# The first weights of a mixture-of-experts kernel: a transfer of its own for chunk 1, and two transfers issued by ScalarE

## The chip, the cores and the metric

One core of one Trainium2 chip. The metric is the device time of the kernel in microseconds (us); lower is better. Everything here happens once, in the first 11 us of about 309.

## The reference

Two steps on x of shape (16, 128, 128), with residuals. The first is a mixture of 8 routed experts and a shared one, each a gated pair of projections; the second multiplies each of the 16 blocks from the left with one of 100 matrices, chosen by a step number.

```python
g = einsum('bsd,edf->ebsf', h, Wg);  u = einsum('bsd,edf->ebsf', h, Wu)
expert_outs = einsum('ebsf,efd->ebsd', silu(g) * u, Wd)          # 8 experts, D = 128, F = 512
expert_output = einsum('be,ebsd->bsd', gating_probs, expert_outs)
shared = einsum('bsf,fd->bsd', silu(h @ Sg) * (h @ Su), Sd)
x = x + (1 - sg) * expert_output + sg * shared
x = x + einsum('bij,bjk->bik', T[steps - 1], x)
```

## The kernel before

The 16 blocks are four tiles `t` of 4 blocks, each 128 x 512 (`W` = 512) with D on the partitions. The 512 hidden features of an expert are four chunks `c` of 128. A unit `n` is one chunk of one expert for one tile: `project_g` and `project_u` make a 128x512 bank each, ScalarE takes SiLU of the first (`silu`), VectorE multiplies (`make_h`), and two units later (`LAG` = 2) `project_down` adds the chunk's part to an output bank. 9 experts x 4 tiles x 4 chunks are 144 units, expert by expert, tile by tile, chunk by chunk.

Each product is made of three matmuls: every operand is split into a rounded high part (`_hi`) and a rest (`_lo`), and hi·hi, hi·lo and lo·hi are added. So a unit is 9 matmuls of 128x512 and the splits are work for the other engines: the high part is a copy to the type fp32r, and the low part is the difference. In the loop GpSimd splits the weights of the next expert. Expert 0 has no expert ahead of it, and its split is written out by hand:

- SyncE issues, in this order: tile 0 of x; gate and up weights of chunk 0 (`W_gu0`, 128 KB); gate and up weights of chunks 1 to 3 (`W_gu`, 384 KB); all down weights (`W_d0`, 256 KB); tile 1 of x; the side values; tiles 2 and 3 of x; all of expert 1.
- ScalarE loads its table, runs one activation on a zero (so that the table is there), rounds chunk 0 (semaphore `w0_rounded` 1), chunk 1 (`w0_rounded` 2), takes SiLU of unit 0, and rounds the down weights (`w0_rounded` 3).
- VectorE rounds and splits tile 0 of x, makes the low part of chunk 1 and the high part of chunks 2 and 3 (`split_done` 3, which is `EARLY`).
- GpSimd makes the low parts of chunk 0, chunk 2, chunk 3 and the down weights, in this order, and counts them in `w_ready` 1 to 4.
- TensorE runs 8 matmuls on a tile of zeros (`warm_up`), then unit 0 (`opening`, each of hi·hi, lo·hi and hi·lo for gate and up), unit 1, and from unit 2 the loop, in which it waits for `w_ready` 2 ahead of unit 2, and for `w_ready` 4 ahead of the first `project_down`.

All engines run their own list in order and wait on semaphores. Nothing is scheduled by a program.

Of the kernel before, what the change touches and what calls it, by code (L numbers as in the profile page):

```python
# [5 lines left out]
P = 128  # L6
F32 = mybir.dt.float32
# [5 lines left out]
def moe_then_step_kernel(  # L13
# [3 lines left out]
    step: bass.AP,  # L17
    W_gu0: bass.AP,
    W_gu: bass.AP,
    W_d0: bass.AP,  # L20
# [8 lines left out]
    NC = W_all.shape[2]  # L29
# [10 lines left out]
    LAG = 2  # L40
# [16 lines left out]
    with ExitStack() as ctx:  # L57
# [3 lines left out]
        def sem(name):  # L61
            return ctx.enter_context(nc.semaphore(name))

        zero = sb("zero", [P, P])
        x_hi = sb("x_hi", [P, NT, W], F32R)
        x_lo = sb("x_lo", [P, NT, W], F32R)
        w_raw = sb("w_raw", [P, 2, NC, 3, P])
        w_hi = sb("w_hi", [P, 2, NC, 3, P], F32R)
# [17 lines left out]
        g_bank = [ctx.enter_context(nc.psum_tensor(f"g_bank{i}", [P, W], F32)) for i in range(2)]  # L86
# [3 lines left out]
        x_in = [sem(f"x_in{i}") for i in range(3)]  # L90
        wc0_in = [sem(f"wc0_in{i}") for i in range(2)]
        wd0_in = sem("wd0_in")
# [52 lines left out]
        def _(sp):  # L145
# [6 lines left out]
            load_x(0, 1, x_in[0])  # L152
            sp.dma_start(w_raw[:, 0, 0, 0:2, :], W_gu0[:, :, :]).then_inc(wc0_in[0], 16)
            sp.dma_start(w_raw[:, 0, 1:NC, 0:2, :], W_gu[:, :, :, :]).then_inc(wc0_in[1], 16)
            sp.dma_start(w_raw[:, 0, :, 2, :], W_d0[:, :, :]).then_inc(wd0_in, 16)
# [42 lines left out]
        def _(pool):  # L198
# [5 lines left out]
            def low_part(slot, c, m):  # L204

                return nc.gpsimd.tensor_tensor(w_lo[:, slot, c, m, :], w_raw[:, slot, c, m, :],  # L206
                                               w_hi[:, slot, c, m, :].bitcast(F32), ALU.subtract)
# [7 lines left out]

            pool.wait_ge(w0_rounded, 1)
            low_part(0, 0, slice(0, 2)).then_inc(w_ready, 1)
            pool.wait_ge(split_done, EARLY)
            low_part(0, 2, slice(0, 2)).then_inc(w_ready, 1)
            low_part(0, 3, slice(0, 2)).then_inc(w_ready, 1)  # L220
            pool.wait_ge(w0_rounded, 3)
            low_part(0, slice(0, NC), 2).then_inc(w_ready, 1)

# [57 lines left out]
        def _(act):  # L281
# [22 lines left out]
            def round_w0(c, m):  # L304
                nc.scalar.activation(w_hi[:, 0, c, m, :], w_raw[:, 0, c, m, :], ACT.Copy).then_inc(w0_rounded, 1)  # L305

            act.wait_ge(zero_done, 1)
            nc.scalar.activation(silu_0[:, :], zero[:, 0:1], ACT.Silu)
            for c in range(2):
                act.wait_ge(wc0_in[c], 16)  # L310
                round_w0(c, slice(0, 2))
            silu(0, 0)
# [26 lines left out]
        def _(dve):  # L339
# [30 lines left out]
            def copy_result(i):  # L370
# [9 lines left out]
            nc.vector.tensor_tensor(x_lo[:, 0, :], acc[:, 0, :], x_hi[:, 0, :].bitcast(F32), ALU.subtract).then_inc(split_done, 1)  # L380
            dve.wait_ge(w0_rounded, 2)
            nc.vector.tensor_tensor(w_lo[:, 0, 1, 0:2, :], w_raw[:, 0, 1, 0:2, :], w_hi[:, 0, 1, 0:2, :].bitcast(F32),
                                    ALU.subtract).then_inc(split_done, 1)
            dve.wait_ge(wc0_in[1], 16)
            nc.vector.tensor_copy(w_hi[:, 0, 2:NC, 0:2, :], w_raw[:, 0, 2:NC, 0:2, :]).then_inc(split_done, 1)
# [45 lines left out]
        def _(pe):  # L431
# [64 lines left out]
            def warm_up(n):  # L496

                for _ in range(n):
                    nc.tensor.matmul(o_bank[1][:, 0:P], zero[:, :], zero[:, :], start=True, stop=True)

            pe.wait_ge(zero_done, 1)
            warm_up(8)

            def opening(x_part, w_part, start, stop):
                for bank, m in ((g_bank[0], 0), (u_bank[0], 1)):
                    last = nc.tensor.matmul(bank[:, :], w_part[:, 0, 0, m, :], x_part[:, 0, :], start=start, stop=stop)
                    if stop:
                        last.then_inc(u_done if m else g_done, 1)

            pe.wait_ge(x_rounded, 1)  # L510
            pe.wait_ge(w0_rounded, 1)
            opening(x_hi, w_hi, True, False)
            pe.wait_ge(split_done, 1)
            opening(x_lo, w_hi, False, False)
            pe.wait_ge(w_ready, 1)
            opening(x_hi, w_lo, False, True)
            pe.wait_ge(w0_rounded, 2)
            nc.tensor.matmul(g_bank[1][:, :], w_hi[:, 0, 1, 0, :], x_hi[:, 0, :], start=True, stop=False)
# [4 lines left out]
            with pe.Fori(0, E - 2, 2) as e:  # L523
                for k in range(LAG, 2 * U + LAG):

                    if k in (2, 3):
                        pe.wait_ge(w_ready, k)
                    if k % U == 0:
                        pe.wait_ge(w_ready, NC * (e + k // U + 1))
                    if k in range(NC, U, NC):  # L530
                        pe.wait_ge(acc_done, k // NC)
                    project_g(e * U + k, k, place(k))
                    project_u(e * U + k, k, place(k))
                    if k == LAG:

                        pe.wait_ge(w_ready, NC)
                    project_down(e * U + k - LAG, k - LAG, place(k - LAG))
# [77 lines left out]
```

## Time and profile before

| | us |
|---|---|
| time before, median of 3 runs | 308.99 (308.96 to 309.49) |
| the profiled execution: its own time | 309.61 |
| the profiled execution: its span in the trace | 307.8 |
| TensorE (PE) busy | 303.3 of 307.8 |

The trace is of one execution. Its span runs from the first to the last record; 1.81 us of the execution's own time lie around it. PE is the matmul, PEld TensorE's load of weights (it overlaps PE), DVE is VectorE, ACT ScalarE, POOL GpSimd, SPq SyncE's queue of DMA issues. Matmuls are pipelined: a 128x512 matmul is shown with about 0.39 us, while the next one starts 0.23 us after it; the distance of starts is the one to count.

### The profile page before, as it was taken

To read this page: it belongs to the slowest core of one execution; us is meant where nothing else is said; L and a number is where in the kernel's file an instruction comes from. 1 tells how busy PE (TensorE), PEld (TensorE's weight loads), DVE (VectorE), ACT (ScalarE), POOL (GpSimd) and SP (SyncE) were. 2 spreads that over 40 slices of the span, in tenths; PEclk is the share of its full clock that TensorE was granted. 3 is DMA by queue.
4 is the path that set the end of the run, shared out by engine and by line. 5 is a ranking of instruction groups with operands and counts; after the bars stand their busy time and mean duration, and the time that the engine had idled before them with its cause. 6 is when DMAs were issued, how large, how long until landed. Compare 5 with 4: busy or idle time off the path is not lost.

```text
span 307.8 us, 4474 instructions
## 1 busy us (share of the span) xinstructions
PE 303.3 (99%) x1348; PEld 251.0 (82%) x1348; DVE 214.4 (70%) x350; ACT 162.4 (53%) x301; POOL 102.5 (33%) x116
## 2 busy tenths in 40 slices
PE   8999999999999999999999999999999999999996
PEld 7788888888888888888888888888888888888885
DVE  2667766776676666776677667776676667787974
ACT  4665555555555555555555555555555555554562
POOL 2675212441155115511542134411451155710010
PEclk9999999999999999999999999999999999999999
DMA  7600300030002000020003000003000000013242
GB/s 201 252 2 0 103 1 2 0 102 0 1 0 86 16 0 0 6 97 0 0 0 111 26 26 26 19 25 111 0 0 2 0 0 0 2 34 68 39 101 102
DMA packets 13882, 12.00 MB, mean 39 GB/s; under 512 B 6960, under 2 KB 11952, under 8 KB 13872
## 3 DMA queue, kind: packets, MB, share of 16 engines
q1 hardware_dynamic: 13872, 11.87, 12.6%
q8 instruction: 6, 0.10, 0.1%
q14 instruction: 4, 0.03, 0.0%
HBM read 10.04 MB, written 1.84 MB: 39 GB/s over the span
## 4 chain that ended last, share of the span: by engine, by line
PE 95%; DMA 2%; POOL 1%; DVE 1%; SPq 0%; issue 0%; ACT 0%
PE o_bank L461 11%; PE o_bank L464 11%; PE o_bank L462 11%; PE g_bank L434 10%; PE u_bank L434 10%; PE g_bank L436 10%; PE u_bank L436 10%; PE g_bank L435 10%; PE u_bank L435 10%; DMA w_raw<-in_W_gu 2%; POOL w_lo L206 1%; PE o_bank L479 1%; DVE res L373 1%; PE g_bank L479 0%; PE u_bank L474 0%
## 5 line engine op out<-in xcount | busy, mean ns | idle before, releaser
L344 DVE TENSOR_TENSOR u_bank<-u_bank,silu_g 128x512 f32<-128x512 f32 x144 | 100.7, 699 | 83.4 <-PE u_bank L436 83.3
L286 ACT ACTIVATE silu_g<-g_bank 128x512 f32<-128x512 f32 x144 | 86.1, 598 | 134.3 <-PE g_bank L436 134.2
L249 POOL TENSOR_TENSOR acc<-acc,scaled 128x512 f32<-128x512 f32 x32 | 41.5, 1298 | 183.4 <-DVE scaled L358 183.2
L350 DVE TENSOR_TENSOR h_lo<-u_bank,h_hi 128x512 fp32r<-128x512 f32 x144 | 97.9, 680 | 0.1
L292 ACT ACTIVATE h_hi<-u_bank 128x512 fp32r<-128x512 f32 x144 | 85.4, 593 | 0.4 <-DVE u_bank L344 0.4
L461 PE MATMUL o_bank<-h_hi,w_hi 128*128 128x512 f32 x144 | 56.2, 390 | 0.2 <-POOL w_lo L206 0.2
L464 PE MATMUL o_bank<-h_lo,w_hi 128*128 128x512 f32 x144 | 56.0, 389 | 0.0
L462 PE MATMUL o_bank<-h_hi,w_lo 128*128 128x512 f32 x144 | 56.0, 389 | 0.0
L436 PE MATMUL u_bank<-x_hi,w_lo 128*128 128x512 f32 x143 | 55.6, 389 | 0.0
L434 PE MATMUL u_bank<-x_hi,w_hi 128*128 128x512 f32 x143 | 55.6, 389 | 0.0
L435 PE MATMUL u_bank<-x_lo,w_hi 128*128 128x512 f32 x143 | 55.6, 389 | 0.0
L434 PE MATMUL g_bank<-x_hi,w_hi 128*128 128x512 f32 x142 | 55.4, 390 | 0.0
L435 PE MATMUL g_bank<-x_lo,w_hi 128*128 128x512 f32 x142 | 55.3, 389 | 0.0
L436 PE MATMUL g_bank<-x_hi,w_lo 128*128 128x512 f32 x142 | 55.2, 389 | 0.0
L206 POOL TENSOR_TENSOR w_lo<-w_raw,w_hi 128x384 fp32r<-128x384 f32 (+2 forms) x36 | 36.2, 1009 | 7.9 <-ACT w_hi L305 2.8
L461 PEld LDWEIGHTS o_bank<-h_hi,w_hi 128*128 128x128 f32 x144 | 27.0, 188 | 6.1 <-POOL w_lo L206 0.6
L464 PEld LDWEIGHTS o_bank<-h_lo,w_hi 128*128 128x128 f32 x144 | 27.0, 188 | 5.7
L462 PEld LDWEIGHTS o_bank<-h_hi,w_lo 128*128 128x128 f32 x144 | 27.0, 188 | 5.5
L434 PEld LDWEIGHTS g_bank<-x_hi,w_hi 128*128 128x128 f32 x142 | 26.7, 188 | 5.9 <-ACT silu_g L286 0.5
L436 PEld LDWEIGHTS u_bank<-x_hi,w_lo 128*128 128x128 f32 x143 | 26.8, 188 | 5.6
L435 PEld LDWEIGHTS u_bank<-x_lo,w_hi 128*128 128x128 f32 x143 | 26.8, 188 | 5.6
L434 PEld LDWEIGHTS u_bank<-x_hi,w_hi 128*128 128x128 f32 x143 | 26.8, 188 | 5.5
(58 smaller groups left out, 143.9 us busy)
## 6 DMA issues: line engine op xcount, KB each, us to landing
w_raw<-in_W_all SPq DMA_DIRECT2D x8, 768.0 KB, 4.4
T_plus<-in_TT SPq DMA_DIRECT2D x16, 64.0 KB, 1.7
turned_y<-yB SPq DMA_DIRECT2D x3, 256.0 KB, 2.3
y<-turned_y SPq DMA_DIRECT2D x12, 64.0 KB, 2.3
out_y<-res SPq DMA_DIRECT2D x3, 256.0 KB, 2.2
acc<-in_xT SPq DMA_DIRECT2D x2, 256.0 KB, 3.8
acc<-in_xT SPq DMA_DIRECT2D x1, 512.0 KB, 6.7
w_raw<-in_W_gu SPq DMA_DIRECT2D x1, 384.0 KB, 4.8
```

What stands on the lines that cost most here:

```text
L206: return nc.gpsimd.tensor_tensor(w_lo[:, slot, c, m, :], w_raw[:, slot, c, m, :], w_hi[:, slot, c, m, :].bitcast(F32), ALU.subtract)
L249: nc.gpsimd.tensor_tensor(acc[:, t, :], acc[:, t, :], scaled[:, t % 2, :], ALU.add).then_inc(acc_done, 1)
L286: nc.scalar.activation(silu_g[:, k % 2, :], g_bank[k % 2][:, :], ACT.Silu).then_inc(g_read, 1)
L292: nc.scalar.activation(h_hi[:, k % HR, :], u_bank[k % HR][:, :], ACT.Copy).then_inc(h_rounded, 1)
L344: nc.vector.tensor_tensor(u_bank[k % HR][:, :], u_bank[k % HR][:, :], silu_g[:, k % 2, :], ALU.mult).then_inc(h_done, 1)
L350: nc.vector.tensor_tensor(h_lo[:, k % HR, :], u_bank[k % HR][:, :], h_hi[:, k % HR, :].bitcast(F32), ALU.subtract).then_inc(split_done, 1)
L434: nc.tensor.matmul(bank, w_hi[:, w[0], w[1], w[2], :], x_h, start=start, stop=False)
L435: nc.tensor.matmul(bank, w_hi[:, w[0], w[1], w[2], :], x_l, start=False, stop=False)
L436: return nc.tensor.matmul(bank, w_lo[:, w[0], w[1], w[2], :], x_h, start=False, stop=stop)
L461: nc.tensor.matmul(bank[:, :], w_hi[:, w[0], w[1], w[2], :], h_hi[:, slot, :], start=c == 0, stop=False)
L462: nc.tensor.matmul(bank[:, :], w_lo[:, w[0], w[1], w[2], :], h_hi[:, slot, :], start=False, stop=False)
L464: last = nc.tensor.matmul(bank[:, :], w_hi[:, w[0], w[1], w[2], :], h_lo[:, slot, :], start=False, stop=c == NC - 1)
```

## The change

Chunk 1 gets a tensor and a transfer of its own, and `W_gu` shrinks to chunks 2 and 3. ScalarE issues the transfer of chunk 0 and that of chunks 2 and 3 itself, ahead of its table load; SyncE issues x tile 0, chunk 1, the down weights and the rest. Chunk 0 is rounded in two halves (gate, then up), and the first two matmuls wait for one half each, so that every later count of `w0_rounded` is one more. GpSimd makes the low part of the down weights ahead of that of chunk 3, and TensorE's waits follow: `w_ready` 2 ahead of unit 2, 3 ahead of the first `project_down`, 4 ahead of unit 3. The warm-up matmuls read a constant zero, which the program's preamble sets on GpSimd, and no longer wait for VectorE's `zero`.

```diff
@@ SyncE
             load_x(0, 1, x_in[0])
-            sp.dma_start(w_raw[:, 0, 0, 0:2, :], W_gu0[:, :, :]).then_inc(wc0_in[0], 16)
-            sp.dma_start(w_raw[:, 0, 1:NC, 0:2, :], W_gu[:, :, :, :]).then_inc(wc0_in[1], 16)
+            sp.dma_start(w_raw[:, 0, 1, 0:2, :], W_gu1[:, :, :]).then_inc(wc0_in[1], 16)
             sp.dma_start(w_raw[:, 0, :, 2, :], W_d0[:, :, :]).then_inc(wd0_in, 16)
@@ GpSimd
-            pool.wait_ge(w0_rounded, 1)
+            pool.wait_ge(w0_rounded, 2)
             low_part(0, 0, slice(0, 2)).then_inc(w_ready, 1)
             pool.wait_ge(split_done, EARLY)
             low_part(0, 2, slice(0, 2)).then_inc(w_ready, 1)
+            pool.wait_ge(w0_rounded, 4)
+            low_part(0, slice(0, NC), 2).then_inc(w_ready, 1)
             low_part(0, 3, slice(0, 2)).then_inc(w_ready, 1)
-            pool.wait_ge(w0_rounded, 3)
-            low_part(0, slice(0, NC), 2).then_inc(w_ready, 1)
@@ ScalarE
+            act.dma_start(w_raw[:, 0, 0, 0:2, :], W_gu0[:, :, :]).then_inc(wc0_in[0], 16)
+            act.dma_start(w_raw[:, 0, 2:NC, 0:2, :], W_gu[:, :, :, :]).then_inc(wc0_in[2], 16)
             act.wait_ge(zero_done, 1)
             nc.scalar.activation(silu_0[:, :], zero[:, 0:1], ACT.Silu)
-            for c in range(2):
-                act.wait_ge(wc0_in[c], 16)
-                round_w0(c, slice(0, 2))
+            act.wait_ge(wc0_in[0], 16)
+            for m in range(2):
+                round_w0(0, m)
+            act.wait_ge(wc0_in[1], 16)
+            round_w0(1, slice(0, 2))
@@ VectorE
-            dve.wait_ge(w0_rounded, 2)
+            dve.wait_ge(w0_rounded, 3)
...
-            dve.wait_ge(wc0_in[1], 16)
+            dve.wait_ge(wc0_in[2], 16)
@@ TensorE
-                    nc.tensor.matmul(o_bank[1][:, 0:P], zero[:, :], zero[:, :], start=True, stop=True)
-
-            pe.wait_ge(zero_done, 1)
+                    nc.tensor.matmul(o_bank[1][:, 0:P], nought, nought, start=True, stop=True)
+
+            nought = nc.const_aps.tensor(0.0, (P, P), F32)
             warm_up(8)
...
-            pe.wait_ge(w0_rounded, 1)
-            opening(x_hi, w_hi, True, False)
+            for bank, m in ((g_bank[0], 0), (u_bank[0], 1)):
+                pe.wait_ge(w0_rounded, m + 1)
+                nc.tensor.matmul(bank[:, :], w_hi[:, 0, 0, m, :], x_hi[:, 0, :], start=True, stop=False)
...
-                    if k in (2, 3):
-                        pe.wait_ge(w_ready, k)
+                    if k == LAG:
+                        pe.wait_ge(w_ready, 2)
+                    if k == LAG + 1:
+                        pe.wait_ge(w_ready, NC)
...
                     if k == LAG:
-                        pe.wait_ge(w_ready, NC)
+                        pe.wait_ge(w_ready, 3)
                     project_down(e * U + k - LAG, k - LAG, place(k - LAG))
```

The first place is the start of ScalarE's list. Before (`in_W_gu0` is chunk 0, `w_hi<-w_raw` the rounding of weights, `silu_g<-g_bank` the SiLU of a unit):

```order
L308 ACT_TABLE_LOAD
L308 ACTIVATE silu_0<-zero 128x1 [waits zero_done]
L305 ACTIVATE w_hi<-w_raw 128x256 [waits wc0_in0]
L305 ACTIVATE w_hi<-w_raw 128x256 [waits wc0_in1]
L286 ACTIVATE silu_g<-g_bank0 128x512 [waits g_done]
L305 ACTIVATE w_hi<-w_raw 128x4x128 [waits wd0_in]
L286 ACTIVATE silu_g<-g_bank1 128x512 [waits g_done]
```

And after the change:

```order
L307 DMA w_raw<-in_W_gu0 128x256
L308 DMA w_raw<-in_W_gu 128x2x256
L310 ACT_TABLE_LOAD
L310 ACTIVATE silu_0<-zero 128x1 [waits zero_done]
L305 ACTIVATE w_hi<-w_raw 128x128 [waits wc0_in0]
L305 ACTIVATE w_hi<-w_raw 128x128
L305 ACTIVATE w_hi<-w_raw 128x256 [waits wc0_in1]
L286 ACTIVATE silu_g<-g_bank0 128x512 [waits g_done]
L305 ACTIVATE w_hi<-w_raw 128x4x128 [waits wd0_in]
L286 ACTIVATE silu_g<-g_bank1 128x512 [waits g_done]
```

Two DMA issues now stand ahead of the table load, and the rounding of chunk 0 is two instructions.

The second place is GpSimd's list from its first low part (`w_lo<-w_raw,w_hi`) on. Before, the four rows are chunk 0, chunk 2, chunk 3 and the down weights (128x4x128):

```order
L206 TENSOR_TENSOR w_lo<-w_raw,w_hi 128x256 [waits w0_rounded]
L206 TENSOR_TENSOR w_lo<-w_raw,w_hi 128x256 [waits split_done]
L206 TENSOR_TENSOR w_lo<-w_raw,w_hi 128x256
L206 TENSOR_TENSOR w_lo<-w_raw,w_hi 128x4x128 [waits w0_rounded]
L227 TENSOR_TENSOR x_lo<-acc,x_hi 128x512 [waits x_rounded]
```

And after the change:

```order
L206 TENSOR_TENSOR w_lo<-w_raw,w_hi 128x256 [waits w0_rounded]
L206 TENSOR_TENSOR w_lo<-w_raw,w_hi 128x256 [waits split_done]
L206 TENSOR_TENSOR w_lo<-w_raw,w_hi 128x4x128 [waits w0_rounded]
L206 TENSOR_TENSOR w_lo<-w_raw,w_hi 128x256
L227 TENSOR_TENSOR x_lo<-acc,x_hi 128x512 [waits x_rounded]
```

The down weights' row has moved up past chunk 3's, so chunk 3 now also stands behind ScalarE's rounding of the down weights.

## Rows read from the trace of the kernel before

**Rows 1.** Busy time by stretch (PE, PEld, DVE, ACT, POOL), granted clock, DMA share, GB/s.

```profile
4.50:10.53 6.03, 5.48 (x20) 3.49 (x20) 2.96 (x7) 3.90 (x8) 3.53 (x5) 1.00 0.99 333
10.53:303.69 293.16, 293.16 (x1306) 243.08 (x1307) 208.82 (x338) 156.10 (x289) 98.08 (x106) 1.00 0.10 30
```

**Rows 2.** Who PE waited for from 11 us (of 308) on: total, times, longest.

```profile
PE o_bank L461 <- POOL w_lo L206: 0.2, 1, 0.2
```

**Rows 3.** Timeline of TensorE, 0 to 11 us: start, duration, what, wait before.

```profile
1.06 3.78 PE L499 MATMUL o_bank<-zero 128*128 128x128 f32 x16 [1.06 <-DVE zero L376]
...
4.50 0.77 PE L506 MATMUL g_bank<-x_hi,w_hi 128*128 128x512 f32 x1
...
5.07 0.63 PE L506 MATMUL u_bank<-x_hi,w_hi 128*128 128x512 f32 x1
...
5.50 0.48 PE L506 MATMUL g_bank<-x_lo,w_hi 128*128 128x512 f32 x1
...
6.05 0.40 PE L506 MATMUL g_bank<-x_hi,w_lo 128*128 128x512 f32 x1
...
6.28 0.39 PE L506 MATMUL u_bank<-x_hi,w_lo 128*128 128x512 f32 x1
...
6.97 0.50 PE L518 MATMUL g_bank<-x_hi,w_hi 128*128 128x512 f32 x1 [0.29 <-ACT w_hi L305]
...
8.67 0.49 PE L434 MATMUL g_bank<-x_hi,w_hi 128*128 128x512 f32 x1
...
10.53 0.50 PE L461 MATMUL o_bank<-h_hi,w_hi 128*128 128x512 f32 x1 [0.21 <-POOL w_lo L206]
```

**Rows 4.** The chain that ended last, 0 to 11 us: start, duration, what.

```profile
1.66 4.82 DMA w_raw<-in_W_gu
...
7.29 0.43 DVE w_hi L385
...
7.79 2.70 POOL w_lo L206 x3
```

**Rows 5.** Timeline of the other engines, 0 to 11 us.

```profile
0.75 1.28 ACT L308 ACT_TABLE_LOAD   x1 [0.75 <-PEq L604]
...
3.54 0.43 DVE L378 CAST x_hi<-acc 128x512 fp32r<-128x512 f32 x1 [2.53 <-DMA acc<-in_xT]
...
3.83 0.42 ACT L305 ACTIVATE w_hi<-w_raw 128x256 fp32r<-128x256 f32 x1 [1.58 <-DMA w_raw<-in_W_gu]
4.00 0.69 DVE L380 TENSOR_TENSOR x_lo<-acc,x_hi 128x512 fp32r<-128x512 f32 x1
...
7.30 0.62 ACT L305 ACTIVATE w_hi<-w_raw 128x512 fp32r<-128x512 f32 x1
```

**Rows 6.** Timeline of SyncE's issues: start, duration of the issue.

```profile
1.18 0.43 SPq L153 DMA_DIRECT2D w_raw<-in_W_gu  x1
...
1.66 0.64 SPq L154 DMA_DIRECT2D w_raw<-in_W_gu  x1
...
2.34 0.61 SPq L155 DMA_DIRECT2D w_raw<-in_W_d  x1
```

**Rows 7.** DMA issues, 0 to 12 us: KB each, us from issue to landing.

```profile
w_raw<-in_W_gu SPq DMA_DIRECT2D x1, 384.0 KB, 4.8
w_raw<-in_W_d SPq DMA_DIRECT2D x1, 256.0 KB, 4.9
w_raw<-in_W_gu SPq DMA_DIRECT2D x1, 128.0 KB, 2.6
```

**Rows 8.** GpSimd's low parts of weights, 0 to 12 us: ns min/median/max.

```profile
L206 POOL TENSOR_TENSOR w_lo<-w_raw,w_hi x4: 736/850/1290, 4.3 to 9.2; 128x256 fp32r<-128x256 f32 x3, 128x512 fp32r<-128x512 f32 x1
```

**Rows 9.** The page, costliest groups: busy us, mean ns of one, idle before.

```profile
L286 ACT ACTIVATE silu_g<-g_bank 128x512 f32<-128x512 f32 x144 | 86.1, 598 | 134.3 <-PE g_bank L436 134.2
```

**Rows 10.** Busy time by stretch, as rows 1; last column GB/s.

```profile
2.50:3.00 0.50, 0.50 (x5) 0.50 (x4) 0.00 (x0) 0.00 (x0) 0.00 (x0) 1.00 1.04 387
...
3.50:4.00 0.50, 0.50 (x4) 0.50 (x3) 0.43 (x1) 0.17 (x1) 0.00 (x0) 1.00 0.81 154
```

More of the change, by code:

```diff
@@ L18, in moe_then_step_kernel @@
     W_gu0: bass.AP,
+    W_gu1: bass.AP,
     W_gu: bass.AP,
@@ L90, in moe_then_step_kernel @@
         x_in = [sem(f"x_in{i}") for i in range(3)]
-        wc0_in = [sem(f"wc0_in{i}") for i in range(2)]
+        wc0_in = [sem(f"wc0_in{i}") for i in range(3)]
         wd0_in = sem("wd0_in")
@@ L516, in _ @@
             opening(x_hi, w_lo, False, True)
-            pe.wait_ge(w0_rounded, 2)
+            pe.wait_ge(w0_rounded, 3)
             nc.tensor.matmul(g_bank[1][:, :], w_hi[:, 0, 1, 0, :], x_hi[:, 0, :], start=True, stop=False)
@@ L597 @@
         "W_gu0": routed[0, :, 0, 0:2],
-        "W_gu": routed[0, :, 1:, 0:2],
+        "W_gu1": routed[0, :, 1, 0:2],
+        "W_gu": routed[0, :, 2:, 0:2],
         "W_d0": routed[0, :, :, 2],
```

## The prediction, made before the changed kernel ran

> **What bounds the kernel now.** I read the table by stretch first. From 10.53 us to 303.69 TensorE is busy for 293.16 of 293.16 us [rows 1], and the only wait that the list of waits gives it from 11 us on is one of 0.2 us that belongs to the matmul at 10.53 [rows 2]. So the middle has a fixed length, and what the start gains, the whole kernel gains, if nothing behind it is tied to the clock on the wall instead of to TensorE. In the stretch ahead, 4.50 to 10.53, there is something to gain: 6.03 us [rows 1], for 18 matmuls (units 0, 1 and 2). At full pace they start 0.23 us apart, as 6.28 does after 6.05 [rows 3], which makes 4.1 us. The other 1.9 us are lost.
>
> The chain that ended last says who is to blame: the 384 KB transfer of chunks 1 to 3 from 1.66 to 6.48, behind it VectorE's cast of chunks 2 and 3 at 7.29, then three low parts on GpSimd for 2.70 us, until 10.49 [rows 4]. The timeline of TensorE shows where the 1.9 us lie. Its first two matmuls start 0.57 and 0.43 us apart (4.50, 5.07, 5.50), against 0.23 later [rows 3]; the granted clock reads 1.00 in this stretch [rows 1] and doesn't show this, but the same shape at twice the distance is the 1.2 GHz level against 2.4. The pace changes between 5.50 and 6.05. The four distances from 4.50 to 6.05 are 1.55 us against 0.92: 0.6 us for the low clock. Then 6.28 to 6.97 is 0.46 too long (chunk 1 wasn't there), with another 0.1 behind it; unit 2 starts at 8.67, 0.2 late with 0.1 behind it, for GpSimd's chunk 2; and 10.53 is 0.38 late, for GpSimd's last low part [rows 3]. The idle pieces sum to 1.26 us.
>
> **The start of the first matmul.** The warm-up runs from 1.06 for 3.4 us, up to 4.50, and it waited for VectorE's zero tile until 1.06 [rows 3]. ScalarE's list starts at 0.75 [rows 5]; TensorE's would start about then too, so the warm-up, if it costs the same, ends at 4.2 instead of 4.5: 0.30 us. That the same 8 matmuls on a constant that is read again and again are no slower, no row shows; I take them as equal, bounded by nothing gained at all (0) and the full 0.3. Is the first operand there at 4.2? x tile 0 landed at 3.54, its cast takes 0.43, so 3.97 [rows 5]. Chunk 0 landed 2.6 us after its issue at 1.18 [rows 6, 7]; issued at 0.75 by ScalarE that is 3.35. ScalarE itself has to issue twice (0.43 and at most 0.64, from SyncE's rows [rows 6]) and load its table (1.28 [rows 5]), which ends at 3.1, plus the activation on one column, about 3.35. Then two halves; a whole 256 takes 0.42 [rows 5], so the gate half is there by 3.7 and the up half by 4.0. I count 0.30.
>
> **The clock.** If the rise stays at about 5.65 us, starting 0.3 earlier only buys 0.3 us at half pace, 0.15 of it is lost again. If it moves with the warm-up, nothing is. The row shows one rise, 4.6 us after the first warm-up matmul [rows 3]. The Trainium skill, "TensorE: Matmul & The Clock Gate", section "What's actually happening", says that the chip's activity monitor doesn't restart with the kernel and that the moment of the rise varies by some 500 ns from run to run. By that rule the rise keeps no distance to the warm-up, and the sum would be 1.4 instead of 1.55, with a scatter of 0.25 us around it; one trace can't tell.
>
> **Chunk 1.** Alone it is 128 KB, issued second by SyncE at 1.18; the 128 KB that stood there landed after 2.6 us, at 3.8 [rows 6, 7]; at worst 4.8 as the 384 KB did, at 6.0. Rounding is 0.42. From 4.2, 3.4 matmuls at half pace bring TensorE to 5.65, and the rest of unit 0 to 6.25. So chunk 1 may land at 5.8 without being felt, and the 0.56 us of idleness there goes.
>
> **Chunks 2 and 3.** 256 KB, issued at 1.2 instead of 1.66. Even at the 4.8 us of the larger transfer they are there at 6.0. Behind them: cast 0.43 on VectorE [rows 4], low part of chunk 2 0.74 [rows 8], 7.2 us. TensorE comes to unit 2 at 6.25 + 6 x 0.23 = 7.6. The 0.31 us there go, with 0.4 to spare.
>
> **Down weights and the new order on GpSimd.** Issued at 1.66 instead of 2.34; at 4.9 us they land at 6.6 [rows 6, 7]. ScalarE has SiLU of unit 0 ahead of them, until about 6.8, and rounds in 0.62 [rows 5]: 7.4. GpSimd then takes 1.29 [rows 8], 8.7, and chunk 3 another 0.74, 9.45. TensorE wants the first at 7.6 + 1.4 = 9.0, and chunk 3 three matmuls later, at 9.7. Both fit, by 0.3 and 0.25; in the old order both would be wanted at 9.0 and the later of them be there at 9.2. The 0.38 us go. If the down weights land no earlier than now (7.24), GpSimd ends them at 9.2 and 0.2 us come back; that is the bound of this term.
>
> What else is late next: the first project_down also wants unit 0 from ScalarE and VectorE. A ScalarE step on 128x512 takes 0.60 [rows 9], one of VectorE 0.69, as x_lo did [rows 5]. SiLU of unit 1 then ends at about 7.9, the rounding of unit 0's product at 8.5, VectorE's split of it, behind its make_h of unit 1, at 9.3; the third matmul of project_down would want it at 9.45. It fits. GpSimd's low part of x tile 1 (wanted by unit 4 at 11.8) would end at 10.8. Transfers for later are issued earlier by 0.6 us or more. The low part of chunk 0 now lies beside all of VectorE's x_lo; if one has to wait for the other, 0.74 + 0.69 [rows 5, 8] from 4.0 is 5.45, and it is wanted at 5.7. Nothing for either.
>
> **Sum.** 0.30 + 0.56 + 0.31 + 0.38 = 1.55; minus up to 0.15 for the clock. I take 1.5: the span goes from 307.8 to 306.3, the profiled execution from 309.61 to 308.1. That execution lies 0.6 above the median of the runs; against the median 308.99 the forecast is 307.5. About 0.2% (0.6 us) is what a measurement of this kernel can tell from no change.
>
> **Rivals.**
> First, the transfers get in each other's way at the start. x tile 0 was alone in front of its queue; now chunk 0, and behind it chunks 2 and 3, start beside it. What speaks against a price: between 3.5 and 4.0 the DMA engines moved only 154 GB/s, against 387 between 2.5 and 3.0 [rows 10], so there was room. What speaks for one: if x shares half and half, 256 KB of other data go before its end, 0.68 us at 387 GB/s; it lands at 4.2, its cast ends at 4.65, and the first matmul is at 4.7, not 4.2. The gain is 1.0, and with x late by a part of that, 1.0 to 1.3: a time of 307.7 to 308.0, and up to 308.4 if ScalarE's own issues are slower than SyncE's as well. The page "DMA: Bandwidth & Descriptors", section "Queues, rings and completion order", of the Trainium skill has this rule: each DMA engine goes round the queues that have work, packet by packet. It would make the late x of this rival the rule and the gain 1.0.
>
> Second, and slower: the clock. The warm-up ends 0.3 us earlier, x comes later, and TensorE stands idle for half a microsecond ahead of its first real matmul, when the clock hasn't risen yet. If that pushes the rise back, each matmul at the low clock costs 0.20 us more. It decides at 1.5 / 0.20 = 7 to 8 further slow matmuls, a rise at about 8.9 us instead of 5.65. If it doesn't rise before the first project_down, 14 to 15 matmuls cost 2.9, and the time is 309.0 - 1.5 + 2.9 = 310.4. For it: the trace has no idle stretch ahead of the rise, so nothing shows that one is harmless. Against it: the needed gap takes a late x, and 0.4 us idle are little beside 3.4 of warm-up.
>
> Third, no change that shows: something outside the span eats it. 1.81 us of the profiled execution lie there; a second engine with a queue of transfers might add to them, by 0.9 us or more for this rival. The time would be 308.4 to 309.6. No row speaks for it.
>
> **Chances.** The forecast (306.9 to 307.9) 0.66; the first rival (307.7 to 308.4) 0.14; the third 0.10; the second 0.10, most of it above 309.6. Range: 306.9 to 308.6, which is the forecast and the first rival. Faster by over 0.2%: 0.80. Within it: 0.11. Slower: 0.09.
>
> **What would show it.** Right: the warm-up starts at about 0.75; the first 128x512 matmul at 4.2; no idle time between units 0 and 1; unit 2 at 7.6 and the first project_down at 9.0 instead of 10.53; from there TensorE without a gap, and a span of 306.3. Wrong: x tile 0 cast later than 3.9; distances of 0.43 us beyond 6 us; the first project_down released by GpSimd after 9.3; a span that shrinks while the time doesn't; any new wait of TensorE behind 11 us.

## The result: half of the forecast time, though the trace moved by almost all of it

| | before | after |
|---|---|---|
| median of 16 runs each, us | 309.18 (308.49 to 309.62) | 308.35 (307.91 to 309.22) |
| profiled execution, its time and span | 309.61, 307.8 | 308.21, 306.4 |

The ratio is 0.9976 (95% interval 0.9969 to 0.9983): the change makes the kernel faster by 0.24%, 0.74 us, with 0.5 to 1.0 us in the interval; the two medians are 0.83 us apart. 1.5 us were forecast, so the size is off by a factor of two. 308.35 lies inside the range of 306.9 to 308.6, but in the part that belongs to the first rival and not in that of the forecast, which ends at 307.9. The two profiled executions differ by 1.4 us, in span and in time alike.

The page of the changed kernel, its head and its shares by engine of the chain that ended last:

```profile
span 306.4 us, 4476 instructions
PE 98%; DVE 1%; issue 0%
```

The chain itself, from its start to the first matmul of project_down (start, duration, what):

```profile
0.78 3.75 PE o_bank L503 x16
4.54 0.59 PE g_bank L517
...
9.15 0.50 PE o_bank L465
```

The transfer, the cast and the three low parts of [rows 4] are gone; the chain is TensorE from 0.78 us on, but for one wait of TensorE's load of weights for GpSimd that comes up below. (The chain counts from end to end and the timeline from start to start, so the first matmul is at 4.54 here and at 4.47 there.) The timeline, which answers to [rows 3]:

```profile
0.78 3.75 PE L503 MATMUL o_bank<-const-float32-0.0 128*128 128x128 f32 x16 [0.78 <-PEq L612]
...
4.47 0.65 PE L517 MATMUL g_bank<-x_hi,w_hi 128*128 128x512 f32 x1
...
4.96 0.40 PE L517 MATMUL u_bank<-x_hi,w_hi 128*128 128x512 f32 x1
...
5.20 0.40 PE L510 MATMUL g_bank<-x_lo,w_hi 128*128 128x512 f32 x1
...
5.97 0.39 PE L510 MATMUL u_bank<-x_hi,w_lo 128*128 128x512 f32 x1
...
6.20 0.40 PE L523 MATMUL g_bank<-x_hi,w_hi 128*128 128x512 f32 x1
...
7.58 0.39 PE L438 MATMUL g_bank<-x_hi,w_hi 128*128 128x512 f32 x1
...
8.72 0.39 PE L440 MATMUL u_bank<-x_hi,w_lo 128*128 128x512 f32 x1
...
9.15 0.50 PE L465 MATMUL o_bank<-h_hi,w_hi 128*128 128x512 f32 x1
```

Units 0, 1 and 2 follow each other without a gap: 5.97, 6.20, and unit 2 at 7.58. Behind unit 2 a gap of 0.2 us is left: its last matmul is at 8.72, and project_down 0.43 us later instead of 0.23. The first project_down is at 9.15 instead of 10.53: 1.38 us, which is the whole difference of the spans. But the first matmul is at 4.47, no earlier than before (4.50), though the warm-up began 0.28 us earlier. The same stretch on the other engines, which answers to [rows 5, 6]:

```profile
0.75 0.42 ACTq L307 DMA_DIRECT2D w_raw<-in_W_gu  x1
...
1.20 0.60 ACTq L308 DMA_DIRECT2D w_raw<-in_W_gu  x1
...
1.83 1.28 ACT L310 ACT_TABLE_LOAD   x1 [1.83 <-issue]
...
3.83 0.43 DVE L382 CAST x_hi<-acc 128x512 fp32r<-128x512 f32 x1 [2.83 <-DMA acc<-in_xT]
...
4.02 0.82 ACT L305 ACTIVATE w_hi<-w_raw 128x128 fp32r<-128x128 f32 x3 [0.69 <-DMA w_raw<-in_W_gu]
...
4.61 0.97 POOL L206 TENSOR_TENSOR w_lo<-w_raw,w_hi 128x256 fp32r<-128x256 f32 x1 [3.13 <-ACT w_hi L305]
4.90 0.96 DVE L386 TENSOR_TENSOR w_lo<-w_raw,w_hi 128x256 fp32r<-128x256 f32 x1
...
7.08 0.63 ACT L305 ACTIVATE w_hi<-w_raw 128x512 fp32r<-128x512 f32 x1 [0.31 <-DMA w_raw<-in_W_d]
...
7.79 1.99 POOL L206 TENSOR_TENSOR w_lo<-w_raw,w_hi 128x512 fp32r<-128x512 f32 x2 [0.77 <-ACT w_hi L305]
```

x tile 0 is cast at 3.83 instead of 3.54, and chunk 0, issued 0.43 us earlier than before, is rounded at 4.02 instead of 3.83. Both operands of the first matmul are later. The landing times, which answer to [rows 7], say it of chunk 0 and chunk 1:

```profile
w_raw<-in_W_gu ACTq DMA_DIRECT2D x1, 256.0 KB, 3.9
w_raw<-in_W_d SPq DMA_DIRECT2D x1, 256.0 KB, 5.4
w_raw<-in_W_gu ACTq DMA_DIRECT2D x1, 128.0 KB, 3.2
w_raw<-in_W_gu SPq DMA_DIRECT2D x1, 128.0 KB, 3.2
```

128 KB took 2.6 us before, and take 3.2 us now. The down weights took 4.9 and take 5.4, so that they land at 7.05, 0.2 us earlier for an issue that is 0.7 us earlier; ScalarE waits for them (0.31), GpSimd behind it, and the first project_down starts when the low part of the down weights is there, at 9.1. The list of waits names it, for TensorE's load of weights:

```profile
PEld o_bank L465 <- POOL w_lo L206: 0.5, 1, 0.5
```

### The profile page after: what moved, and what is told of

It is laid out like the page before. It is cut to its first block, busy times and chain, and to the rows that moved or that the text cites. A ratio compares the mean times of both kernels' runs of the same rounds, so it can differ in the third digit from the quotient of the medians.

```text
span 306.4 us, 4476 instructions
## 1 busy us (share of the span) xinstructions
PE 302.7 (99%) x1348; PEld 250.9 (82%) x1348; DVE 214.9 (70%) x350; ACT 162.5 (53%) x302; POOL 102.3 (33%) x116
## 4 chain that ended last, share of the span: by engine, by line
PE 98%; DVE 1%; issue 0%
PE o_bank L465 11%; PE o_bank L466 11%; PE o_bank L468 11%; PE u_bank L439 11%; PE u_bank L440 11%; PE u_bank L438 11%; PE g_bank L439 11%; PE g_bank L440 11%; PE g_bank L438 10%; PE o_bank L503 1%; PE o_bank L483 1%; DVE res L377 1%; PE g_bank L483 0%; PE g_bank L517 0%; PE g_bank L510 0%; PE u_bank L510 0%
```

## The experiments

All ratios are against the kernel before, run beside each version on the same chip. "First matmul" is the first of 128x512, "project_down" the first matmul of the first project_down.

**The two kernels again** (e1, e2, e13, e16), and the two parts of the change that can be separated without moving a transfer. e3 is the kernel before with only the new warm-up:

```diff
-                    nc.tensor.matmul(o_bank[1][:, 0:P], zero[:, :], zero[:, :], start=True, stop=True)
-            pe.wait_ge(zero_done, 1)
+                    nc.tensor.matmul(o_bank[1][:, 0:P], nought, nought, start=True, stop=True)
+            nought = nc.const_aps.tensor(0.0, (P, P), F32)
```

e4 is the changed kernel with the same edit taken back.

> The kernel before, unchanged, to see how far one execution lies from the next. Theory A (the profiled execution of before was a slow draw of its opening): the first project_down starts earlier than 10.53 us, by up to 0.6, because the low clock ends sooner or a transfer lands sooner, and the span is 307.2 to 307.6. Theory B (the gain inside the span is real, 1.4 us, and something outside the span gives half of it back): the first project_down again at 10.5, span 307.8, and time minus span is smaller here than in the changed kernel by 0.5. Ratio 1.000.

> The changed kernel, unchanged. Theory A: first project_down at 9.1 to 9.6, span 306.4 to 306.9, time minus span 1.8 as in the kernel before. Theory B: time minus span above 2.3. Ratio about 0.997 to 0.998.

> The kernel before with one part of the change: the warm-up reads the constant and doesn't wait for VectorE. By the prediction's sum this part alone is worth 0.3 us if the first matmul follows the end of the warm-up: warm-up from 0.78, first 128x512 matmul at 4.25 instead of 4.50, ratio 0.999. Rival: the chain behind it (chunk 1's transfer, GpSimd's low parts) sets the first project_down, so the start gains nothing: ratio 1.000, first project_down still at 10.1 to 10.5.

> The changed kernel without that part: the warm-up waits for VectorE's zero tile again. In the changed kernel's trace the first matmul waited for x at 4.44, past the end of the warm-up at about 4.2, so if the transfers set the start, this costs 0.1 us or less (warm-up ends 4.5): ratio 0.998. Rival: the earlier warm-up brings the earlier clock, then this costs 0.3 us: distances of 0.43 us last until 5.6 and the ratio is 0.999.

> The changed kernel once more. Cast of x between 3.8 and 4.1, span between 306.0 and 307.1 by where the clock rises (the first project_down at 9.1 with a rise before 5.2, at 9.5 to 9.8 with one behind 6), ratio 0.998.

> The kernel before once more. Cast of x at 3.2 to 3.6, rounding of chunk 1 at 6.0 to 6.5, the first project_down 4.0 us behind that start, whatever the clock does: 10.0 to 10.5, span 307.0 to 307.8, ratio 1.000.

| | ratio (95%) | x cast | first matmul | full pace from about | project_down | span |
|---|---|---|---|---|---|---|
| before, profiled first | | 3.54 | 4.50 | 5.7 | 10.53 | 307.8 |
| e1 before | 1.000 (0.9991 to 1.0009) | 3.46 | 4.38 | 4.5 | 10.23 | 307.5 |
| e16 before | 1.000 (0.9991 to 1.0009) | 3.56 | 4.49 | 6.0 | 10.17 | 307.4 |
| e3 only the constant | 0.9992 (0.9983 to 1.0001) | 3.55 | 4.41 | 4.5 | 10.59 | 307.8 |
| after, profiled first | 0.9976 (0.9969 to 0.9983) | 3.83 | 4.47 | 4.9 | 9.15 | 306.4 |
| e2 after | 0.9980 (0.9971 to 0.9989) | 3.99 | 4.63 | 6.6 | 9.79 | 306.9 |
| e13 after | 0.9969 (0.9957 to 0.9981) | 4.00 | 4.66 | 4.8 | 9.13 | 306.3 |
| e4 after, old warm-up | 0.9979 (0.9969 to 0.9989) | 3.96 | 4.60 | 5.2 | 9.07 | 306.2 |

Theory B (something outside the span takes half back) falls: in every execution of every kernel here the time is the span plus 1.75 to 1.89 us. Theory A holds in part. The 33 executions of the kernel before that ran beside e1 have spans from 306.8 to 308.0, with a median of 307.4; the profile that the prediction read, with 307.8, took 0.4 more than that. The 16 of the changed kernel span 306.1 to 307.4 with a median of 306.55, and its profile, with 306.4, lies a little below. So two traces that differ by 1.4 stand for medians that differ by 0.8.

What scatters is told by the columns. In the kernel before, project_down comes 4.03 or 4.04 us behind the start of chunk 1's rounding in all three profiles, and in e3's. In e1 and e16, by the timeline:

```profile
6.20 0.42 ACT L305 ACTIVATE w_hi<-w_raw 128x256 fp32r<-128x256 f32 x1 [2.05 <-DMA w_raw<-in_W_gu]
...
10.23 0.50 PE L461 MATMUL o_bank<-h_hi,w_hi 128*128 128x512 f32 x1 [0.22 <-POOL w_lo L206]
```

```profile
6.13 0.42 ACT L305 ACTIVATE w_hi<-w_raw 128x256 fp32r<-128x256 f32 x1 [1.87 <-DMA w_raw<-in_W_gu]
...
10.17 0.50 PE L461 MATMUL o_bank<-h_hi,w_hi 128*128 128x512 f32 x1 [0.21 <-POOL w_lo L206]
```

(first e1, then e16). The clock went up at 4.5 in one and at about 6.0 in the other, and the sum doesn't care. In the changed kernel it does: e2 and e13 are the same program with x cast within 0.01 us, in neither does TensorE wait at project_down, and e2's is 0.66 later, because its matmuls kept half pace until 6.47. e2 by the timeline, and e13's first two matmuls and project_down behind it:

```profile
4.63 0.77 PE L517 MATMUL g_bank<-x_hi,w_hi 128*128 128x512 f32 x1
...
5.19 0.63 PE L517 MATMUL u_bank<-x_hi,w_hi 128*128 128x512 f32 x1
...
6.04 0.63 PE L510 MATMUL u_bank<-x_lo,w_hi 128*128 128x512 f32 x1
6.47 0.49 PE L510 MATMUL g_bank<-x_hi,w_lo 128*128 128x512 f32 x1
...
7.04 0.40 PE L523 MATMUL g_bank<-x_hi,w_hi 128*128 128x512 f32 x1
...
9.79 0.39 PE L465 MATMUL o_bank<-h_hi,w_hi 128*128 128x512 f32 x1
```

```profile
4.66 0.47 PE L517 MATMUL g_bank<-x_hi,w_hi 128*128 128x512 f32 x1
...
4.97 0.40 PE L517 MATMUL u_bank<-x_hi,w_hi 128*128 128x512 f32 x1
...
9.13 0.39 PE L465 MATMUL o_bank<-h_hi,w_hi 128*128 128x512 f32 x1
```

A second thing scatters in the changed kernel, the landing of the down weights. They take 5.4 us in the first profile and 5.8 in e5's, which differs only in GpSimd's order, and there the matmul of project_down waits for GpSimd by 0.2 and 0.36 us; they take 4.5 us in e2, e4 and e13, and nothing waits.

e3 and e4 say that the earlier warm-up is worth nothing that shows: 0.9992 with an interval that just holds 1, where 0.3 us would be 0.9990, and e4, without it, lies on the changed kernel. The ratio of e3 by itself would allow the 0.3 us; what speaks against them is its profile, in which the first matmul comes 0.1 us earlier at most and chunk 1's landing still sets project_down, at 10.59. In the changed kernel x is late for the end of the warm-up; in the kernel before chunk 1 is late for the end of unit 0.

**The order on GpSimd** (e5), the changed kernel with chunk 3 ahead of the down weights again:

```diff
+            low_part(0, 3, slice(0, 2)).then_inc(w_ready, 1)
             pool.wait_ge(w0_rounded, 4)
             low_part(0, slice(0, NC), 2).then_inc(w_ready, 1)
-            low_part(0, 3, slice(0, 2)).then_inc(w_ready, 1)
...
-                        pe.wait_ge(w_ready, 3)
+                        pe.wait_ge(w_ready, NC)
```

> The changed kernel with GpSimd's old order: low part of chunk 3 ahead of that of the down weights, and the old count at the first project_down. The prediction had the new order pay for part of its 0.38 us. Theory L (what holds the first project_down is the landing of the down weights, at 7.05 to 7.45, and their rounding behind it): chunk 3's low part fits into the gap that GpSimd has there anyway, the low part of the down weights still starts at 7.8, and nothing changes: ratio to the kernel before 0.998. Rival O (the order matters): the first project_down 0.5 to 0.7 us later and ratio 0.9995 to 1.000.

Ratio 0.9977 (0.9968 to 0.9986), as the changed kernel, so the rival O falls and theory L holds. By e5's timeline:

```profile
6.45 1.44 POOL L206 TENSOR_TENSOR w_lo<-w_raw,w_hi 128x256 fp32r<-128x256 f32 x2 [0.70 <-DVE w_hi L389]
...
7.43 0.63 ACT L305 ACTIVATE w_hi<-w_raw 128x512 fp32r<-128x512 f32 x1 [0.47 <-DMA w_raw<-in_W_d]
...
8.14 1.29 POOL L206 TENSOR_TENSOR w_lo<-w_raw,w_hi 128x512 fp32r<-128x512 f32 x1 [0.25 <-ACT w_hi L305]
...
9.49 0.50 PE L465 MATMUL o_bank<-h_hi,w_hi 128*128 128x512 f32 x1 [0.20 <-POOL w_lo L206]
```

Chunks 2 and 3 are through at 7.89, ahead of the end of ScalarE's rounding at 8.06. The low part of the down weights starts when it may, in either order, and what is late is the weights. Where they land early, as in e13 (ScalarE is through with them at 7.45, GpSimd with chunk 2 at 7.19), an estimate from e13's rows has the old order end them at 7.19 + 0.74 + 1.29 = 9.22, 0.1 us behind TensorE's 9.13. That is too little for these ratios to show.

**How much of the low clock is hidden** (e7, e8): `warm_up(8)` becomes `warm_up(4)` in the kernel before (e7) and in the changed one (e8).

> The kernel before with 4 warm-up matmuls instead of 8, so that the low clock lasts longer. Theory K (in the kernel before the low clock of the opening is hidden behind the wait for chunk 1, in the changed one it is exposed): units 0 at half pace end before or about the arrival of chunk 1 at 6.2 to 6.7; the time rises by less than 0.5 us, ratio 1.000 to 1.0015. Rival: the clock counts equally in both, and this and the same edit of the changed kernel cost the same.

> The changed kernel with 4 warm-up matmuls instead of 8. Theory K: every matmul at half pace costs 0.2 us in full, the first project_down is 0.6 to 1.5 us later than in the changed kernel, ratio to the kernel before 1.000 to 1.002, clearly more lost than by the same edit in the kernel before. Rival: as much lost as there.

The kernel before takes 309.82 instead of 309.31 (1.0020, 1.0009 to 1.0030), 0.5 us more; the changed kernel 310.04 (1.0019, 1.0005 to 1.0033), which is 1.5 us above the 308.5 that e5, its equal, has beside it. With the low clock lasting until about 9.1 in e7's profile and 10.4 in e8's, theory K holds in kind: what one kernel hides behind its wait for chunk 1 the other one pays. Two sizes were missed: e7 costs 0.5 us, where less was expected, and e8's project_down at 11.53 is 2 us behind e5's 9.49, where 0.6 to 1.5 were. And the kernel before hides the low clock only as long as it ends before chunk 1 is there: in e7 project_down comes 4.60 us behind chunk 1's rounding, at 10.68, instead of 4.03. With 4 warm-up matmuls the two aren't told from each other (309.82 and 310.04), and the whole gain of the change is gone.

**The transfers** (e6, e9, e10, e11, e15; e14 is e10 again). All are the changed kernel with other issues. The first on each queue, in order:

```
                SyncE                                          ScalarE
changed         x 0, chunk 1, down, x 1, ...                   chunk 0, chunks 2-3, then the table load
e6              x 0, chunk 1, chunks 2-3, down, x 1, ...       chunk 0, then the table load
e9              x 0, chunk 0, chunk 1, chunks 2-3, down, ...   none
e10, e14        x 0, chunk 0, chunk 1, down, x 1, ...          table load, activation, then chunks 2-3
e11             x 0, chunk 0, down, x 1, ...                   chunk 1, chunks 2-3, then the table load
e15             x 0, chunk 0, chunk 1, down, x 1, ...          chunks 2-3, then the table load
```

The edit of e10 against the changed kernel:

```diff
+            sp.dma_start(w_raw[:, 0, 0, 0:2, :], W_gu0[:, :, :]).then_inc(wc0_in[0], 16)
             sp.dma_start(w_raw[:, 0, 1, 0:2, :], W_gu1[:, :, :]).then_inc(wc0_in[1], 16)
...
-            act.dma_start(w_raw[:, 0, 0, 0:2, :], W_gu0[:, :, :]).then_inc(wc0_in[0], 16)
-            act.dma_start(w_raw[:, 0, 2:NC, 0:2, :], W_gu[:, :, :, :]).then_inc(wc0_in[2], 16)
             act.wait_ge(zero_done, 1)
             nc.scalar.activation(silu_0[:, :], zero[:, 0:1], ACT.Silu)
+            act.dma_start(w_raw[:, 0, 2:NC, 0:2, :], W_gu[:, :, :, :]).then_inc(wc0_in[2], 16)
             act.wait_ge(wc0_in[0], 16)
```

> The changed kernel, but ScalarE issues only chunk 0; chunks 2 and 3 are issued by SyncE behind chunk 1. Theory X (chunks 2 and 3 on a second queue are what makes x tile 0 land 0.3 to 0.45 us late): the cast of x starts at 3.5 to 3.6 instead of 3.8 to 4.0, the first matmul at 4.2 to 4.3; later transfers go out 0.6 us later, so chunk 2 and 3 or the down weights may hold later units: ratio 0.997 to 0.999. Rival C (chunk 0 alone beside x makes it late, or the noise of the transfers): cast of x at 3.8 or later as in the changed kernel.

> The changed kernel with all transfers issued by SyncE: x tile 0, chunk 0, chunk 1, chunks 2 and 3, down weights. Theory Q (any transfer on a second queue beside x tile 0 makes it land about 0.4 us later, and chunk 0 gains nothing by it): cast of x at 3.4 to 3.6, first matmul at 4.2 to 4.3, and as the low part of the down weights then waits for a transfer issued 1.1 us later, the first project_down at 9.2 to 9.6; ratio to the kernel before 0.997 to 0.998. Rival R (ScalarE's issues are what gives the gain): ratio 0.999 to 1.000.

> SyncE issues x tile 0, chunk 0, chunk 1, down weights and the rest; ScalarE issues only chunks 2 and 3, behind its table load, at 2.25 us. Theory Q: cast of x at 3.4 to 3.6, first matmul at 4.2 to 4.3, down weights no later than in the changed kernel, so the first project_down at 8.6 to 9.2, ratio 0.996 to 0.997, faster than the changed kernel by 0.3 us. Rival (x late by chance, not by the second queue): cast of x at 3.8 to 4.0, ratio 0.998.

> SyncE issues x tile 0 and chunk 0 as in the kernel before, ScalarE chunk 1 and chunks 2 and 3 ahead of its table load. Theory Q: whatever lies on the second queue, x lands late: cast at 3.8 to 4.1; chunk 0 too, later than in the changed kernel by 0.2 or more, ratio 0.998 or a little above. Rival (only chunk 0 beside x hurts): cast of x at 3.5.

> The version of e10 again (ScalarE issues only chunks 2 and 3, in its list behind the first activation). Cast of x at 3.4 to 3.6, ratio 0.996 within 0.0005, and 0.3 to 0.6 us below the changed kernel of the same call. If e10 was luck: ratio 0.998.

> e14 with the one issue of ScalarE moved ahead of the table load, so that it goes out at 0.75 instead of 1.05. Theory Q (a transfer that starts beside x makes x late): cast of x at 3.7 to 4.1, and part of the gain of e14 lost, ratio 0.997. Rival (what makes x late is chunk 0 or chunk 1, small transfers, beside it): cast of x at 3.4 to 3.6, ratio 0.996.

| | ratio (95%) | median, us | x cast | chunk 0 rounded | first matmul | project_down |
|---|---|---|---|---|---|---|
| changed (ratio and median of its first 16 runs, profile of e13) | 0.9976 (0.9969 to 0.9983) | 308.35 | 4.00 | 4.21 | 4.66 | 9.13 |
| e6 | 0.9977 (0.9968 to 0.9987) | 308.64 | 4.33 | 4.51 | 4.96 | 9.66 |
| e9 | 0.9959 (0.9946 to 0.9972) | 308.03 | 3.53 | 3.83 | 4.29 | 9.32 |
| e10 | 0.9958 (0.9944 to 0.9971) | 307.74 | 3.42 | 3.70 | 4.19 | 8.91 |
| e11 | 0.9967 (0.9954 to 0.9980) | 308.06 | 3.89 | 4.40 | 4.86 | 9.32 |
| e14 | 0.9966 (0.9954 to 0.9978) | 308.07 | 3.44 | 3.75 | 4.21 | 8.68 |
| e15 | 0.9989 (0.9971 to 1.0007) | 308.43 | 3.57 | 4.65 | 5.11 | 9.36 |

Two ratios came out better than expected, e9's (0.9959 for 0.997 to 0.998) and e11's (0.9967 for 0.998 or above).

Theory X of e6 falls: with chunks 2 and 3 off ScalarE's queue x is cast at 4.33, the latest of all. Chunk 0 alone beside x is enough. Theory Q, as e9 and e10 had it, holds for the transfers: with nothing else going out at 0.75 us, x is cast at 3.42 to 3.53, chunk 0 is rounded at 3.70 to 3.83, and the first matmul starts at 4.19 to 4.29, where the prediction wanted it. The rival R of e9 (ScalarE's issues are the gain) falls too: without any of them the kernel is as fast, 0.9959. e15 against e14 is the cleanest pair, one issue moved from 1.05 to 0.75 us, with one profile of e15. By its timeline:

```profile
0.75 0.62 ACTq L308 DMA_DIRECT2D w_raw<-in_W_gu  x1
...
3.57 0.43 DVE L382 CAST x_hi<-acc 128x512 fp32r<-128x512 f32 x1 [2.56 <-DMA acc<-in_xT]
...
4.65 0.97 ACT L306 ACTIVATE w_hi<-w_raw 128x128 fp32r<-128x128 f32 x3 [1.75 <-DMA w_raw<-in_W_gu]
```

Here x is in time (3.57), against what Q expected, and chunk 0, behind x on its queue, is 0.9 us late. So in these profiles a transfer on a second queue in the first moment delays what goes out beside it, now x and now chunk 0, and the first matmul needs both. The start alone doesn't set the end, though: e9 and e11 have their first matmuls at 4.29 and 4.86 and both reach project_down at 9.32, and e11's ratio isn't told from e14's. Three of e15's twelve executions took 310.0 to 310.5 us, the others 308.3 to 308.5; why is open, and so its ratio says little.

Do the transfers share the DMA engines, or is pace lost as well? The windows from 2 to 3 and from 3 to 4 us (DMA share and GB/s at the end); first the kernel before, then the changed one:

```profile
2.00:3.00 1.00, 1.00 (x7) 1.00 (x6) 0.00 (x0) 0.23 (x2) 0.00 (x0) 1.00 0.80 265
3.00:4.00 1.00, 1.00 (x6) 1.00 (x6) 0.43 (x1) 0.17 (x1) 0.00 (x0) 1.00 0.73 179
```

```profile
2.00:3.00 1.00, 1.00 (x6) 1.00 (x6) 0.00 (x0) 1.00 (x1) 0.00 (x0) 1.00 0.65 204
3.00:4.00 1.00, 1.00 (x7) 1.00 (x6) 0.17 (x1) 0.32 (x2) 0.00 (x0) 1.00 1.08 378
```

And from 2 to 3 us in e6:

```profile
2.00:3.00 1.00, 1.00 (x6) 1.00 (x6) 0.00 (x0) 0.66 (x2) 0.00 (x0) 1.00 0.52 98
```

From 2 to 3 us the DMA engines move 265 to 315 GB/s in the eight profiles in which nothing goes out beside x at 0.75 (the kernel before three times, e3, e7, e9, e10, e14), and 98 to 259 in the ten others (chunk 0 beside x in eight of them, chunk 1 in e11, chunks 2 and 3 in e15). From 3 to 4 us it is the other way round: 328 to 378 GB/s in the ten, 123 to 222 in six of the eight, and 324 and 359 in e10 and e14, whose second queue is at work by then.

What counts for x is how much had been moved in all when it landed. From 1 us to the landing (taken as 0.02 us ahead of the cast) that is 426 kB in the kernel before (169 GB/s for 2.52 us) and 570 kB in the changed one (203 GB/s for 2.81 us); 395 to 448 kB in the eight, 543 to 630 kB in the nine in which x is late, and 485 kB in e15, where it isn't. So where x is late, 100 to 200 kB more of other transfers had gone ahead of its end. At the 378 GB/s of 3 to 4 us the 144 kB between the two kernels are 0.38 us, an estimate, and x is late by 0.29. The DMA engines being shared is therefore enough for the size of the delay in the first profile. In e6 pace is lost as well: x comes 0.5 us later than in the first profile of the changed kernel, with as much moved (576 kB). Why the start is slow with two queues, and why the 0.3 us between e14's issue and e15's matter so much, these rows don't show, and it stays open.

By the timeline of e14, ScalarE and the opening:

```profile
0.74 1.28 ACT L309 ACT_TABLE_LOAD   x1 [0.74 <-PEq L612]
...
1.05 0.63 ACTq L310 DMA_DIRECT2D w_raw<-in_W_gu  x1
...
3.44 0.43 DVE L382 CAST x_hi<-acc 128x512 fp32r<-128x512 f32 x1 [2.43 <-DMA acc<-in_xT]
...
4.21 0.72 PE L517 MATMUL g_bank<-x_hi,w_hi 128*128 128x512 f32 x1
...
8.68 0.39 PE L465 MATMUL o_bank<-h_hi,w_hi 128*128 128x512 f32 x1
```

e10's version has the lowest median: 307.99 us over its 12 executions (e10, e14), against 308.45 for 33 executions of the changed kernel, and 308.03 for the 5 of e9, from which it isn't told. The gap is near the scatter; where it and the changed kernel ran side by side (e13, e14) the medians are 0.08 apart and not told from each other, against the 0.3 to 0.6 that were expected. That the transfers come earlier in these versions is shown; how much of it the time gets is not.

**A longer warm-up** (e12): `warm_up(8)` becomes `warm_up(10)` in the changed kernel.

> The changed kernel with 10 warm-up matmuls instead of 8, which fills the idle time between the end of the warm-up at 4.2 and the first operand at 4.4. Theory G (that idle time pushes the rise of the clock back): the slow half of the runs disappears, distances of 0.43 us end by 5.2, ratio 0.997. Theory F (the moment of the rise has nothing to do with it): the two more matmuls push the opening back by 0.2 to 0.4 us in part of the runs, ratio 0.998 to 0.999.

Ratio 0.9976 (0.9966 to 0.9986), as the changed kernel, with the first matmul at 5.04 and full pace from about 5.8 in its profile. It speaks for neither theory clearly: filling the idle time doesn't gain, and the cost that F expected doesn't show in the ratio, though the first matmul is 0.4 us later. That the idle time of 0.2 to 0.4 us ahead of the first matmul isn't enough by itself to keep the clock low is told by e2 and e13, which both have it, with rises at 6.6 and 4.8.

## What the prediction had right, and the steps that failed

**What bounds the kernel, and that the start is passed on in full.** Right. After 11 us TensorE waits for nothing in the changed kernel; from project_down to the end of the span it is 297.3 us in the profiles of before and of after.

**The idle pieces: 0.56 + 0.31 + 0.38.** The first two are gone in every profile of the changed kernel. Of the third, "The 0.38 us go", 0.2 us stayed in the first profile and 0.36 in e5, for down weights that land late; in e2, e4 and e13 it is gone. Units 1 and 2 start where forecast (6.20 and 7.58 against 6.25 and 7.6), project_down is at 9.15 against 9.0, and the span is 306.4 against 306.3. That this fits so well is luck in part: the start is 0.27 us late, and a clock that happened to rise at 4.9 instead of 5.65 gave it back.

**"I count 0.30" for the start: failed.** The first matmul is at 4.47, 4.63 and 4.66 in three profiles of the changed kernel, against 4.38 to 4.50 before. Measured: nothing, or a loss of 0.1 to 0.2 us. The step took chunk 0's landing as its old 2.6 us from an earlier issue, and x as untouched. This is the first rival, smaller than its full price: x 0.3 to 0.5 late instead of 0.68. The Trainium skill's page "DMA: Bandwidth & Descriptors", section "Queues, rings and completion order", has the queues of SyncE and ScalarE share the same 16 engines in turn. A late x agrees with it: cast at 3.4 to 3.5 us without a second queue beside its start (e9, e14), 3.8 to 4.3 with chunk 0 on one, and 543 to 630 kB moved in all by then against 395 to 448. e15 doesn't: its second queue starts as early, and x is cast at 3.57. The rival's 0.68 us came from an even share at 387 GB/s; the runs show a lower pace from 2 to 3 us (98 to 259 GB/s) and a high one behind it, and the measured delay of 0.3 to 0.5 us is smaller than that price. That the clock rose earlier in the profile of after (4.9 against 5.7) hid the loss where the first two traces were compared.

**The clock: right in kind, mis-weighed.** The prediction allowed up to 0.15 us for a rise that keeps to its own time, and took 0.05 off. The rise came at 4.5, 5.7 and 6.0 before, and at 4.8, 4.9 and 6.6 after: with no order in it that these six show. The page "TensorE: Matmul & The Clock Gate" of the Trainium skill, section "What's actually happening", says that it isn't tied to the kernel's start. The traces agree, with a wider spread than its 500 ns to either side: 1.5 us among the three of the kernel before and 1.8 among the three of the changed one. What was missed is the other side: in the kernel before this scatter is free (e1, e16), in the changed kernel it isn't (e2, e13), up to 0.66 us from one execution to the next.

**"Against the median 308.99 the forecast is 307.5": the step that cost most.** The idle pieces were those of an execution of 309.61, and the text noted the 0.6 us to the median and then took the whole 1.5 off the median. But this distance lay inside the stretch that the change removes: chunk 1 landed at 6.48 in that trace, and at 6.18 and 6.11 in e1 and e16, and project_down moves with it one for one. For the median kernel (span 307.4) project_down is at about 307.4 - 297.3 = 10.1, so the gain to be had is 0.4 us less. The rest lies in the changed kernel: by its median span of 306.55 project_down is at about 9.3, 0.3 us behind the forecast 9.0. The start that gained nothing, the late clock of some executions and the late down weights of others are in it; how the 0.3 us divide among the three isn't measured. 1.5 minus 0.4 minus 0.3 is 0.8, what the medians show.

**Down weights and the new order.** The landing was to be 6.6 and was 7.05 in the first profile and 7.4 in e5, where the bound was 7.24, and about 6.2 in e2, e4 and e13. The order on GpSimd was credited with 0.2 us; e5 shows nothing.

**Rivals.** The first one took a part of the gain. The second one, the idle time that holds the clock down, isn't seen at its price: no rise of the changed kernel is near 8.9 us, and the idle time that e2 and e13 share goes with two different rises. e8, with an idle stretch of 1.8 us and a rise at 10.4, changed the length of the warm-up as well and doesn't tell the two apart. The third one, a cost outside the span, is refuted. Of the signs of being wrong that the prediction named, the first profile shows none; e2 shows two, x cast later than 3.9 and distances of 0.43 us beyond 6 us.

## What to carry to other kernels

Before a gain is read out of one trace, ask which part of the stretch changes from one execution to the next: if it is the very wait that the edit removes, price it from several executions, or the slow trace is counted as gain. A wait removed ahead of TensorE also uncovers what ran hidden beside it; here that was the low clock. And a transfer for which the first matmul waits got nothing here from an earlier issue on a second queue, as what it went out beside was wanted as well: with the first two transfers in one queue, and the second queue starting behind them, x came 0.4 us and chunk 0 0.3 us earlier, or more (e10, e14). That this makes the kernel faster than the change as it stands isn't settled by the runs.

## What the runs showed of the hardware that was not expected

ScalarE's transfer that stands behind its first activation in the program goes out while the table load still runs: issue at 1.05 us, table load from 0.74 to 2.02, activation at 2.04 (e10, e14). Two issues that stand ahead of the table load push it back by their whole length, from 0.75 to 1.83.

VectorE's low part of chunk 1 takes 0.96 us in the changed kernel and 0.43 in the kernel before; it now lies beside GpSimd's low part of chunk 0, which takes 0.97 against the 0.74 of an undisturbed one. Both read two tensors from the on-chip memory. In the kernel before GpSimd's takes 0.96 too, beside VectorE's `x_lo`. In both kernels it ends 0.60 us behind the end of `x_lo`, and VectorE's low part of chunk 1 ends 0.28 us behind GpSimd's end in the changed one: the rows fit each waiting for the other, which no run tested. It cost nothing here that shows: the cast of chunks 2 and 3 behind it started at 5.79, and unit 2 still without a gap.

The granted clock reads 1.00 in stretches in which the matmuls start at half pace (0.43 us apart, as in e2 until 6.47); only the distance of starts shows the level.
